# A graph network's 64-channel table, made for two blocks of nodes at once from unsplit fp32 instead of one block from split bf16

## The chip, the cores and the metric

The kernel runs on one core of one Trainium2 chip. The metric is device time in microseconds (us): the median of three runs, of which the lowest and the highest are also given. One execution was taken with the hardware profiler; every row below is from it.

## The reference, cut to what matters

Four graph layers on 6250 nodes and 100000 edges (`src`, `dst`, sorted by `dst`). The change touches two things that the first and the last layer compute:

```
# layer 0, second convolution: b has 64 channels
agg = segment_sum(b[src], dst)            # "the second sum"
h   = relu((b + agg) @ W1b + b1b) ...
# layer 3, spline convolution of 64 channels, 125 weight matrices of 64 x 64
z        = einsum('ni,kio->nko', v, stn2_w)   # v: nodes x 64; z: nodes x 125 x 64
gathered = z[col*125 + idx]                   # 8 corners of a cell for each edge
out      = segment_sum(sum_s basis * gathered, row) / degree + stn2_b
```

`z` does not depend on the second sum. It is written to HBM as a table, in which cells that are read together lie together, and gathered in a later stage.

## The kernel before

Nodes lie in 49 blocks of 128 (NB), edges in 832 tiles of 128 slots, 8 tiles to a group (T), 104 groups (G), 4 groups to a quad. Every stage is a block of five instruction streams with hand-set semaphores; there is no scheduler, and each engine runs its stream in the written order. All stages follow one another with a barrier between them.

The stage of the change is `second_sum_phase`. It does two jobs side by side:

- **The second sum.** GpSimd (POOL) gathers 128 rows of 384 bytes for each tile by an indirect DMA (L1560) and then issues a small memset (L150). It may gather group g+3 once VectorE has copied that group's indices, which VectorE does (`indices.put`) after it has added the sums of group g-1 into `dest`. TensorE sums a group with 24 bf16 products against one-hot matrices (`sums`, L1641). So gathers run at most some three groups ahead of the sums.
- **The 64-channel table** (`Table`, called `other`). For one block, VectorE splits the fp32 features into three bf16 terms (`three`, 5 instructions), TensorE transposes four stacks of them (`flip`, L1435), ScalarE (ACT) copies these out of PSUM (L1424), and TensorE makes the table in 25 parts of 320 columns: five bf16 products add up to one part in one of five PSUM banks (`multiply`, L1451). ACT copies each part to a staging buffer `z` (L1417); after five parts SyncE (SP) stores a piece of 960 KB (L1370). There are two `z` buffers, and ACT waits until the store of two pieces ago has landed.

TensorE's order for a pair of blocks is: 24 loop rounds, each with flip, 12 parts, sums, 13 parts, sums, and the same again for the other block; so one quad of the sum goes with one pair of blocks. Then come the last block's 25 parts and the sums of the last two quads (groups 96 to 103).

The weights are prepared far earlier, in the sorter's second stage (`place_phase`). There POOL scatters rows with indirect DMAs (L656), VectorE ranks the edges, and at the end of each of its 49 rounds splits a slice of the weights into bf16 terms (`HalfWeights.split`); after the last round SP stores them to HBM (L361 for the 64-channel ones).

Of the kernel before, what the change touches and what calls it, by code (L numbers as in the profile page):

```python
# [297 lines left out]
class HalfWeights:  # L298
# [6 lines left out]
    def __init__(self, k, stn2_w, conv_w, tent_w):  # L305
        self.of = stn2_w, conv_w, tent_w
        self.wide = [dram(k, "wide_w", [LO, self.WIDE], BF16) for _ in range(2)]
        self.slim = dram(k, "slim_w", [LO, self.SLIM + self.TENT], BF16)

    def hold(self, k):  # L310

        self.step_wide, self.step_slim = (-(-n // SPLIT_STEPS) for n in (self.WIDE, self.SLIM + self.TENT))
        self.raw_wide = sb(k, None, "raw_wide", [LO, self.step_wide * SPLIT_STEPS])
        self.raw_slim = sb(k, None, "raw_slim", [LO, self.step_slim * SPLIT_STEPS])
# [3 lines left out]
    def load(self, eng, sem):  # L318
        stn2_w, conv_w, tent_w = self.of
        for n in range(2):  # L320
            to = self.raw_wide[n * D_HID:(n + 1) * D_HID, 0:self.WIDE]
# [8 lines left out]
    def clear(self, dve):  # L330
        dve.memset(self.raw_wide[:, self.WIDE:], 0.0)
# [3 lines left out]
    def parts(self, k, ph):  # L335
        self.halves = [sb(k, ph, "halves", [LO, self.step_wide * SPLIT_STEPS], BF16) for _ in range(2)]
        self.thirds = sb(k, ph, "thirds", [LO, self.step_slim * SPLIT_STEPS], BF16)
# [3 lines left out]
    def split(self, dve, c, i):  # L341
        wide, slim = bass.ds(i * self.step_wide, self.step_wide), bass.ds(i * self.step_slim, self.step_slim)
        w, first, third = self.raw_wide[:, wide], self.halves[0][:, wide], self.halves[1][:, wide]
        v, u = self.raw_slim[:, slim], self.thirds[:, slim]
# [12 lines left out]
        return as_is(dve, u[last_], v[last_])  # L357

    def store(self, eng, sem):
        for n in range(2):  # L360
            eng.dma_start(self.wide[n], self.halves[n][:, 0:self.WIDE]).then_inc(sem, 16)  # L361
        eng.dma_start(self.slim, self.thirds[:, 0:self.SLIM + self.TENT]).then_inc(sem, 16)

    STORES = 16 * 3
# [4 lines left out]
class Sorter:  # L369


    def __init__(self, k):
# [5 lines left out]
        k.halves.hold(k)  # L378
# [19 lines left out]
def load_phase(k, s, src, dst, uv, uvw, s_rows):  # L398
    nc = k.nc
    with phase(nc) as ph:  # L400
# [9 lines left out]
        with nc.Block() as block:  # L410
            @block.sync
            def _(sp):
# [6 lines left out]
                k.halves.load(sp, weighed)  # L419
                sp.wait_ge(weighed, 16 * HalfWeights.LOADS)  # L420
# [12 lines left out]
            def _(dve):  # L433
# [9 lines left out]
                k.halves.clear(dve)  # L443
# [86 lines left out]
def place_phase(k, s, carried, s_rows, d_rows):  # L530
# [3 lines left out]
    with phase(nc) as ph:  # L534
# [8 lines left out]
        k.halves.parts(k, ph)  # L543
# [9 lines left out]
        with nc.Block() as block:  # L553
            @block.vector
            def _(dve):
# [4 lines left out]
                with dve.Fori(0, pairs) as i:  # L560
                    c.enter(i, 2 * 8 + HalfWeights.STEPS)
# [19 lines left out]
                    k.halves.split(dve, c, i).then_inc(split, 1)  # L581
# [39 lines left out]
            def _(sp):  # L621
# [19 lines left out]
                k.halves.store(sp, stored)  # L641
                sp.wait_ge(stored, HalfWeights.STORES)

# [653 lines left out]
class Table:  # L1297
# [8 lines left out]
    def __init__(self, k, ph, src, K, weights, C, rows, side, wide, piece, table, tail=None, shared=False, banks=5, zs=2):  # L1306
# [16 lines left out]
        self.stacks = (0, LO, 2 * LO, K) if K == D_HID else (0, LO, 2 * LO)  # L1323
        self.weights_of = weights
        self.weights = [sb(k, ph, "weights", [LO, rows * side * C], BF16) for _ in weights]
        if K == D_HID:
            first, third = self.weights
            self.terms = ((0, first, LO), (1, first, LO), (2, first, LO), (3, third, LO), (2, third, K))
        else:
            self.terms = tuple((n, self.weights[0], LO) for n in range(3))  # L1330
# [183 lines left out]

class Convolution:
# [3 lines left out]
    def __init__(self, k, K, C):  # L1519
        self.K, self.C = K, C  # L1520
        self.table = dram(k, "corners", [NN * self.CELLS * 25 * self.WIDE, C])

# [43 lines left out]
def second_sum_phase(k, table, dest, making):  # L1566
# [3 lines left out]
    with phase(nc) as ph:  # L1570
# [7 lines left out]
        other = Table(k, ph, *making)  # L1578
        with nc.Block() as block:
# [11 lines left out]
            def _(dve):  # L1591
                c = Chain(dve, own)
                indices.first(dve)
                for n in range(2):
                    other.three(dve, c, other.src[:, n, :], n)
# [13 lines left out]
                def block_ahead(i, b):  # L1609

# [1037 lines left out]
```

## Time and profile before

| | us |
|---|---|
| median of the three runs (lowest, highest) | 11980.05 (11966.1, 11993.72) |
| profiled execution: first to last instruction (span) | 11729.7 |
| median less span | 250.35 |
| stage of the second sum, 3079 to 4648 us of the span | 1569 |
| the same stage: TensorE busy, ACT busy, POOL busy | 1319.9, 574.6, 1032.9 |

The page gives no time of its own for the profiled execution, only its span; what lies outside first and last instruction is taken as the 250.35 us by which the median is longer. Busy times of a stage are to be read against its 1569 us: TensorE is busy for 84% of it, POOL for 66%, ACT for 37%. Busy time of TensorE holds matmuls whose ends are modelled, so the start-to-start distances of groups are the surer measure, and they are used below. Over the whole span TensorE's granted clock averages 0.605 of full speed; in this stage it is 0.87.

### The profile page before, as it was taken

To read this page: it belongs to the slowest core of one execution; us is meant where nothing else is said; L and a number is where in the kernel's file an instruction comes from. 1 tells how busy PE (TensorE), PEld (TensorE's weight loads), DVE (VectorE), ACT (ScalarE), POOL (GpSimd) and SP (SyncE) were. 2 spreads that over 40 slices of the span, in tenths; PEclk is the share of its full clock that TensorE was granted. 3 is DMA by queue.
4 is the path that set the end of the run, shared out by engine and by line. 5 is a ranking of instruction groups with operands and counts; after the bars stand their busy time and mean duration, and the time that the engine had idled before them with its cause. 6 is when DMAs were issued, how large, how long until landed. Compare 5 with 4: busy or idle time off the path is not lost. (4 is left out here: it accounts for less than half of the span.)

```text
span 11729.7 us, 173426 instructions
## 1 busy us (share of the span) xinstructions
PE 6194.3 (53%) x40278; PEld 4754.9 (41%) x40279; DVE 6868.2 (59%) x17651; ACT 2989.3 (25%) x7270; POOL 7301.5 (62%) x10729
## 2 busy tenths in 40 slices
PE   4333244444688987666664555555544444662332
PEld 3222244434344443355553555555523333332222
DVE  6555666664322222577787666666656767655555
ACT  0000022221233332111112555555531111220000
POOL 3888788882366665577773333333327877228887
PEclk8555555555688987566665555555565555685555
DMA  6332222224455554222325777777621111587777
GB/s 195 113 113 57 62 62 62 63 62 131 149 190 187 193 186 134 52 74 74 78 77 147 281 285 278 280 284 281 235 81 43 44 41 43 178 323 219 221 222 199
DMA packets 894930, 1760.69 MB, mean 150 GB/s; under 512 B 487010, under 2 KB 487319, under 8 KB 889928
## 3 DMA queue, kind: packets, MB, share of 16 engines
q0 software_dynamic: 317952, 1023.05, 28.3%
q1 hardware_dynamic: 537672, 598.27, 15.2%
q10 hardware_dynamic: 39168, 138.04, 3.0%
q14 instruction: 113, 0.93, 0.0%
q8 instruction: 25, 0.41, 0.0%
HBM read 1150.36 MB, written 611.50 MB: 150 GB/s over the span
## 5 line engine op out<-in xcount | busy, mean ns | idle before, releaser
L1560 POOL DMA_INDIRECT got<-corners,now x1664 | 1679.5, 1009 | 1926.6 <-DVE now L1548 1171.3
L1560 POOL DMA_INDIRECT got<-node_rows,now x1664 | 1639.6, 985 | 1267.3 <-issue 1251.5
L1451 PE MATMUL made_p<-weights,turned 128*128 128x320 bf16 (+4 forms) x7595 | 1541.8, 334 | 203.0 <-ACT z L1417 106.6
L150 POOL MEMSET spare<- 128x192 f32 x4944 | 1376.4, 278 | 3.1
L2342 PE MATMUL sum_p<-msg_s,hot_s 128*128 128x64 f32 x3328 | 734.2, 422 | 931.6 <-DVE msg_s L1824 931.6
L1560 POOL DMA_INDIRECT got<-patches,now x832 | 839.3, 1009 | 565.4 <-DVE now L1548 283.0
L2342 PEld LDWEIGHTS sum_p<-msg_s,hot_s 128*128 128x128 f32 x3328 | 717.7, 332 | 937.5 <-issue 937.5
L1451 PEld LDWEIGHTS made_p<-weights,turned 128*128 128x128 bf16 (+1 forms) x7595 | 657.9, 101 | 1039.0 <-issue 517.0
L896 POOL DMA_INDIRECT d_rows<-row x832 | 942.9, 1133 | 184.3 <-issue 160.1
L1417 ACT COPY z<-made_p 128x384 f32<-128x384 f32 (+3 forms) x1495 | 714.6, 515 | 932.3 <-PE made_p L1451 612.1
L656 POOL DMA_INDIRECT s_rows<-row_now,pos_i x784 | 848.1, 1082 | 155.2 <-issue 136.5
L1606 DVE TENSOR_TENSOR a<-a,sum_p 128x64 f32 x832 | 184.0, 221 | 1124.4 <-remote 638.0
L1897 PE MATMUL acc_p<-msg,hot_s 128*128 128x32 f32 x1664 | 376.2, 402 | 873.2 <-DVE msg L1841 647.7
L1817 DVE TENSOR_TENSOR got<-got,weight 128x1024 f32<-128x1024 f32 x416 | 481.7, 1220 | 442.0 <-DMA d_rows<-row 422.9
L1897 PEld LDWEIGHTS acc_p<-msg,hot_s 128*128 128x128 f32 x1664 | 362.8, 330 | 887.4 <-issue 887.4
L593 PE MATMUL rank_p<-one,before 128*128 128x100 bf16 x784 | 186.1, 282 | 813.9 <-DVE one L383 743.4
L1831 DVE TENSOR_TENSOR got<-got,spline_w 128x512 f32<-128x512 f32 x416 | 260.8, 688 | 561.9 <-DMA got<-corners,now 561.9
L2441 ACT ACTIVATE prod<-prod,below,alpha 128x32 f32<-128x32 f32 x1664 | 516.4, 398 | 0.0
L864 PE MATMUL sum_p<-basis,hot_s 128*128 128x126 f32 x1664 | 388.2, 427 | 192.0 <-DVE basis L826 192.0
L2425 ACT ACTIVATE hot_d<-column,lo_now 128x128 f32<-128x128 f32 x840 | 256.8, 388 | 889.5 <-PE acc_p L2322 488.7
L864 PEld LDWEIGHTS sum_p<-basis,hot_s 128*128 128x128 f32 x1664 | 359.9, 328 | 211.3 <-DVE basis L826 211.3
L2322 PE MATMUL acc_p<-msg_d,hot_d 128*128 128x32 f32 x1680 | 377.2, 400 | 111.6 <-issue 56.1
(411 smaller groups left out, 13596.3 us busy)
## 6 DMA issues: line engine op xcount, KB each, us to landing
corners<-z SPq DMA_DIRECT2D x245, 960.0 KB
corners<-z SPq DMA_DIRECT2D x98, 864.0 KB
d_rows<-empty ACTq DMA_DIRECT2D x32, 1586.0 KB
row<-d_rows SPq DMA_DIRECT2D x104, 488.0 KB
corners<-z SPq DMA_DIRECT2D x49, 672.0 KB
s_rows<-empty ACTq DMA_DIRECT2D x32, 962.0 KB
row<-s_rows SPq DMA_DIRECT2D x104, 296.0 KB
got<-node_rows,now POOLq DMA_INDIRECT x1664
```

The source lines that it names most:

```text
L150: pool.memset(self.of[:, t, :], 0.0).then_inc(self.cleared, 1)
L656: pool.indirect_dma_start(out=s_rows, out_offset=bass.IndirectOffsetOnAxis(ap=pos_i[b][:, t, 0:1], axis=0), in_=row_now[b][:, t, :], in_of ...
L864: m = nc.tensor.matmul(part(b2, t), hot_s[b2][:, t, :], basis[b2][:, t, :], start=True, stop=True)
L896: pool.indirect_dma_start(out=d_rows, out_offset=bass.IndirectOffsetOnAxis(ap=to[:, t, DPOS:DPOS + 1], axis=0), in_=row[b][:, t, :], in_of ...
L1417: copy(to, of).then_inc(self.out[taker], 1)
L1451: m = nc.tensor.matmul(self.made_p[s % banks][:, 0:w], self.turned[b][0:rows, stack, :], weight[0:rows, at:at + w], start=n == 0, stop=n = ...
L1560: pool.indirect_dma_start(out=to[b][:, t, :], out_offset=None, in_=table, in_offset=bass.IndirectOffsetOnAxis(ap=indices.now[b][:, t:t + 1 ...
L1817: m = dve.tensor_tensor(v, v, last(weights[:, :, 2 * n:2 * n + 2], C), ALU.mult)
L1897: m = nc.tensor.matmul(at_block(acc, block_of(k, pe, t)), hot_s[b2][:, t, :], msg[b2][:, t, :], start=False, stop=False)
L2322: m = nc.tensor.matmul(at_block(acc, block_of(k, pe, t)), hot_d[b2][:, t, :], msg_d[b2][:, t, :], start=False, stop=False)
L2342: m = nc.tensor.matmul(sum_p[b2][:, t, :], hot_s[b2][:, t, :], msg_s[:, n, t, :], start=n == 0, stop=n == 1)
L2441: m = nc.scalar.activation(at[:, n, :], at[:, n, :], ACT.Exp, bias=below[b2][:, n:n + 1], scale=alpha[b2][:, n:n + 1])
```

## The change

`Table` for 64 channels is replaced in this stage by a new class, `PairTable`. Two blocks are taken at once: VectorE copies both blocks' fp32 features side by side (one instruction for ten), one fp32 transpose puts block 0 on partitions 0 to 63 and block 1 on 64 to 127, and each part of each block is then one fp32 product over 64 rows, block 0 from the lower half and block 1 from the upper half, the two in turn. There are four PSUM banks and four `z` buffers; ACT takes part q of block 0, then of block 1. A pair has 50 products instead of 250, 50 ACT copies as before, and 10 stores of 960 KB as before. The weights are kept in fp32, on both halves: the same 4 MB. The other tables (32 channels) keep `Table`.

```diff
 class TableWeights:                      # was HalfWeights
     def split(self, dve, c, i):          # the 64-channel weights are no longer split
-        as_is(dve, first, w)
         c.after(as_is(dve, u, v))
-        dve.tensor_tensor(w, w, first, ALU.subtract)
         c.after(dve.tensor_tensor(v, v, u, ALU.subtract))
-        as_is(dve, third, w)
         as_is(dve, u[second], v[second])
         c.after(as_is(dve, u[last_], v[last_]))
-        as_is(dve, first[D_HID:], third[D_HID:])
-        dve.tensor_tensor(w, w, third, ALU.subtract)
         c.after(dve.tensor_tensor(v[last_], v[last_], u[last_], ALU.subtract))
-        as_is(dve, third, w)
         return as_is(dve, u[last_], v[last_])
...
                         features(i * 2 + b, b, lambda each: T)
+                k.table_w.store_wide(sp, stored)
                 for b in range(2):
...
+class PairTable:
+    PAIRS, PARTS = NB // 2, 25
+    STEPS = 2 * PARTS
+    BANKS, ZS, PIECE = 4, 4, 5
+    BEFORE = (48, 49, 46, 47)
...
+    def store(self, sp, i, blocks=2):
+        cells, unit, rows = self.cells, self.unit, self.PIECE
+        for h, j in self.pieces(blocks):
+            z = (2 * h + j) % self.ZS
+            sp.wait_ge(self.out, i * self.STEPS + (self.STEPS + self.at(h * rows + rows - 1, j, blocks) + 1))
...
+    def pair(self, dve, i):
+        dve.sem_inc(self.seen, 1)
+        dve.tensor_copy(self.now[:], self.src[:, bass.ds(i * 2, 2), :]).then_inc(self.taken, 1)
...
+    def flip(self, pe, i):
+        pe.wait_ge(self.taken, i + 1)
+        pe.sem_inc(self.ready, 1)
+        pe.wait_ge(self.copied, i)
+        of = self.now[:].rearrange("p a k -> p (a k)")
+        self.k.nc.tensor.transpose(self.turned_p[:], of, self.k.ident[:]).then_inc(self.flipped, 1)
+
+    def multiply(self, pe, i, parts, blocks=2):
+        nc, K = self.k.nc, self.K
+        if parts[0] == 0:
+            pe.wait_ge(self.copied, i + 1)
+            pe.sem_inc(self.ready, 1)
+        for q in parts:
+            for j in range(blocks):
+                s = 2 * q + j
+                had = self.STEPS + self.at(q - 2, j, blocks) if q >= 2 else self.BEFORE[s]
+                pe.wait_ge(self.out, i * self.STEPS + (had + 1))
+                rows = slice(j * K, (j + 1) * K)
+                nc.tensor.matmul(self.made_p[s % self.BANKS][:, 0:self.col], self.turned[rows, :],
+                                 self.weights[rows, q * self.col:(q + 1) * self.col], start=True, stop=True).then_inc(self.made, 1)
...
+    def take(self, act, i, blocks=2):
+        C, cells, unit, rows = self.C, self.cells, self.unit, self.PIECE
+        for q, j in self.steps(blocks):
+            h, r = q // rows, q % rows
+            n = 2 * h + j
+            z = self.z[n % self.ZS]
+            if r == 0:
+                act.wait_ge(self.stored[n % self.ZS], i * (16 * self.uses(n % self.ZS)) + 16 * (n // self.ZS))
+                act.sem_inc(self.waited, 1)
+            act.wait_ge(self.made, i * self.STEPS + (self.at(q, j, blocks) + 1))
...
+            self.k.nc.scalar.copy(to, of).then_inc(self.out, 1)
...
 def second_sum_phase(k, table, dest, making):
-        other = Table(k, ph, *making)
+        other = PairTable(k, ph, *making)
...
             def _(pe):
...
-                half = other.parts // 2
-                with pe.Fori(0, NB // 2) as i:
-                    for b in range(2):
-                        n = i * 2 + b
-                        other.flip(pe, n + 1, 1 - b)
-                        other.multiply(pe, n, b, i, range(0, half))
-                        sums(pe, i, b * 2)
-                        other.multiply(pe, n, b, i, range(half, other.parts))
-                        sums(pe, i, b * 2 + 1)
-                other.multiply(pe, NB - 1, 0, NB // 2, range(other.parts))
+                quarters = (0, 7, 13, 19, other.PARTS)
+                with pe.Fori(0, other.PAIRS) as i:
+                    for b in range(4):
+                        other.multiply(pe, i, range(quarters[b], quarters[b + 1]))
+                        if b == 3:
+                            other.flip(pe, i + 1)
+                        sums(pe, i, b)
+                other.multiply(pe, other.PAIRS, range(other.PARTS), 1)
```

How the instructions move is shown by three places of the streams. First TensorE before, at the start of a loop round: `turned_p` are the transposes, `made_p_4488` to `made_p_4492` the five banks.

```order
L1435 MATMUL turned_p<-ident_53,now 128x128 x4
L1448 ISA
L1451 MATMUL made_p_4488<-weights,turned 128x320 x5
L1448 REGISTER_ALU
L1451 MATMUL made_p_4489<-weights,turned 128x320 x5
L1448 REGISTER_ALU
L1451 MATMUL made_p_4490<-weights,turned 128x320 x5
```

And TensorE after, where the first quarter of a pair ends and a group's sums (`sum_p`) follow:

```order
L1603 REGISTER_ALU
L1605 MATMUL made_p_4455<-weights,turned 128x320
L1760 ISA
L124 REGISTER_ALU
L1764 MATMUL sum_p_4422<-got,hot_d 128x64 x24
L1603 REGISTER_ALU
L1605 MATMUL made_p_4456<-weights,turned 128x320
```

A wait now stands before every single product where it stood before five, and the products go round four banks; the sums stand after 14, 12, 12 and 12 products of a pair.

VectorE before, in the last round's code (`now` and `rest` hold the split, `hot_d` the one-hot matrices of the next group):

```order
L1543 COPY now<-src_d 128x8
L1386 CAST now<-v 128x128
L1387 TENSOR_TENSOR rest<-v,now 128x64
L1388 CAST now<-rest 128x128
L1389 TENSOR_TENSOR rest<-rest,now 128x64
L1390 CAST now<-rest 128x128
L228 TENSOR_TENSOR hot_d<-column,lo_d 128x1024
```

VectorE after, in the loop:

```order
L1674 COPY now<-src_d 128x8
L1577 REGISTER_ALU
L1573 ISA
L1573 COPY now<-v 128x128
L228 ISA
L228 TENSOR_TENSOR hot_d<-column,lo_d 128x1024
```

Five instructions have become one, and it comes once in four groups instead of once in two.

SP in the sorter's second stage, before and then after, around the store of the weights (`row_now` are the feature loads of the last two groups):

```order
L627 DMA row_now<-in_edge_attr_2x_dram 80x8x64
L627 DMA row_now<-in_edge_attr_2x_dram 48x8x64
L627 DMA row_now<-in_edge_attr_2x_dram 80x6x64
L627 DMA row_now<-in_edge_attr_2x_dram 48x4x64
L361 DMA wide_w<-halves 128x8000 x2
L362 DMA slim_w<-thirds 128x4512
```

```order
L351 DMA wide_w<-raw_wide 128x8000
L619 DMA row_now<-in_edge_attr_2x_dram 80x8x64
L619 DMA row_now<-in_edge_attr_2x_dram 48x8x64
L619 DMA row_now<-in_edge_attr_2x_dram 80x6x64
L619 DMA row_now<-in_edge_attr_2x_dram 48x4x64
```

The 4 MB of 64-channel weights are now stored ahead of the last two groups' feature loads instead of behind them.

## Rows read from the trace of the kernel before

**Rows 1.** Windows of the second-sum stage: length, busy of each engine (instructions), clock, DMA.

```profile
3079.00:4648.00 1569.00, 1319.91 (x8818) 610.28 (x8818) 387.14 (x1297) 574.55 (x1274) 1032.93 (x1664) 0.87 0.54 182
```

**Rows 2.** Lines by form of that stage: busy us, mean ns, idle before, releasers.

```profile
L1451 PE MATMUL made_p<-weights,turned 128*128 128x320 bf16 x4900 | 974.9, 325 | 159.7 <-ACT z L1417 82.4 <-issue 77.1
L1417 ACT COPY z<-made_p 128x384 f32<-128x384 f32 x1225 | 548.4, 488 | 760.2 <-PE made_p L1451 522.0 <-DMA d_rows<-row 119.4 <-DMA corners<-z 70.4
L1560 POOL DMA_INDIRECT got<-node_rows,now x832 | 805.8, 968 | 889.0 <-issue 887.2 <-POOL spare L150 1.6 <-DMA got<-node_rows,now 0.2
```

**Rows 3.** Waits, 3090 to 4600, ACT and POOL: us in total, times, longest.

```profile
ACT z L1417 <- PE made_p L1451: 522.0, 585, 5.9
...
POOL got L1560 <- issue: 514.5, 797, 11.6
```

**Rows 4.** Timeline, one block in the middle: start, us, engine, line, what.

```profile
4046.92 0.87 PE L1641 MATMUL sum_p<-got,hot_d 128*128 128x64 bf16 x24
...
4047.99 9.45 SPq L1370 DMA_DIRECT2D corners<-z  x2
...
4051.77 0.59 ACT L1424 COPY turned<-turned_p 128x512 bf16<-128x512 bf16 x1 [4.27 <-DMA d_rows<-row]
...
4054.63 2.90 ACT L1417 COPY z<-made_p 128x384 f32<-128x384 f32 x7 [2.27 <-DMA d_rows<-row]
...
4055.16 2.97 PE L1451 MATMUL made_p<-weights,turned 128*128 128x320 bf16 x14 [2.81 <-ACT z L1417]
```

**Rows 5.** Timeline, start and end of the stage (27 calls of L1560 apart, then 29).

```profile
3081.26 1.04 POOL L1560 DMA_INDIRECT got<-node_rows,now  x1 [368.49 <-issue]
...
3094.18 12.36 PE L1451 MATMUL made_p<-weights,turned 128*128 128x320 bf16 x60
...
3119.63 0.95 POOL L1560 DMA_INDIRECT got<-node_rows,now  x1 [0.17 <-issue]
...
4560.35 22.27 PE L1451 MATMUL made_p<-weights,turned 128*128 128x320 bf16 x125
...
4591.35 0.95 POOL L1560 DMA_INDIRECT got<-node_rows,now  x1 [0.16 <-issue]
...
4634.08 0.95 POOL L1560 DMA_INDIRECT got<-node_rows,now  x1 [0.17 <-issue]
...
4641.87 1.46 PE L1641 MATMUL sum_p<-got,hot_d 128*128 128x64 bf16 x24 [11.46 <-DMA got<-node_rows,now]
...
4648.10 3.43 DVE L1234 TENSOR_TENSOR a<-a,b 128x3136 f32<-128x3136 f32 x1 [1.15 <-PEq L79]
```

**Rows 6.** Timeline of TensorE in two dense stages: products of fp32, two records each.

```profile
4661.83 1.17 PE L1098 MATMUL made_p<-stage,weight 128*128 128x256 f32 x2
4662.79 0.64 PE L1083 MATMUL in_p<-ident,a 128*128 128x128 f32 x2
...
4727.89 2.08 PE L1109 MATMUL out_p<-weight,stage 128*128 128x512 f32 x2
4729.75 0.42 PE L1083 MATMUL in_p<-ident,h 128*128 128x128 f32 x1
...
4727.89 0.50 PEld L1109 LDWEIGHTS out_p<-weight,stage 128*128 128x128 f32 x2 [1.50 <-issue]
```

**Rows 7.** Windows of the dense stages and of a later table stage.

```profile
4660.00:4670.00 10.00, 9.59 (x31) 6.93 (x30) 0.86 (x3) 2.31 (x7) 0.00 (x0) 0.50 0.00 0
4729.00:4739.00 10.00, 9.29 (x12) 2.59 (x11) 1.38 (x2) 0.53 (x2) 0.00 (x0) 0.50 0.00 0
10200.00:10300.00 100.00, 87.94 (x469) 42.93 (x470) 63.19 (x150) 46.74 (x87) 0.00 (x0) 0.97 0.97 384
```

**Rows 8.** The page: the rows that the sorter scatters.

```profile
L656 POOL DMA_INDIRECT s_rows<-row_now,pos_i x784 | 848.1, 1082 | 155.2 <-issue 136.5
```

**Rows 9.** Timeline, the end of that stage.

```profile
1339.24 0.83 SPq L361 DMA_DIRECT2D wide_w<-halves  x2
...
1357.73 0.27 POOL L150 MEMSET spare<- 128x192 f32 x1
```

More of the change, by code:

```diff
@@ L377, in __init__ @@
         self.run = sb(k, None, "run", [LO, 2 * KEYS])
-        k.halves.hold(k)
+        k.table_w.hold(k)
     def one_hots(self, k, dve, g, b):
@@ L418, in _ @@
                 sp.wait_ge(loaded, 128)
-                k.halves.load(sp, weighed)
-                sp.wait_ge(weighed, 16 * HalfWeights.LOADS)
+                k.table_w.load(sp, weighed)
+                sp.wait_ge(weighed, 16 * TableWeights.LOADS)
             @block.scalar
@@ L442, in _ @@
                 dve.memset(s.key[:, NE:, :], 0.0)
-                k.halves.clear(dve)
+                k.table_w.clear(dve)
                 dve.wait_ge(loaded, 128)
@@ L542, in place_phase @@
         empty = sb(k, ph, "empty", [LO, FILL, D_W])
-        k.halves.parts(k, ph)
+        k.table_w.parts(k, ph)
         hot, ranked, own, placed, headed, seen, fetched, drawn, filled, split, stored = ph.sems(
@@ L640, in _ @@
                 sp.wait_ge(split, pairs)
-                k.halves.store(sp, stored)
-                sp.wait_ge(stored, HalfWeights.STORES)
+                k.table_w.store_slim(sp, stored)
+                sp.wait_ge(stored, TableWeights.STORES)
             @block.gpsimd
@@ L1322, in __init__ @@
         self.copies = LO // K
-        self.stacks = (0, LO, 2 * LO, K) if K == D_HID else (0, LO, 2 * LO)
+        self.stacks = (0, LO, 2 * LO)
         self.weights_of = weights
         self.weights = [sb(k, ph, "weights", [LO, rows * side * C], BF16) for _ in weights]
[L1326 to L1330, printed above, removed]
+        self.terms = tuple((n, self.weights[0], LO) for n in range(3))
         self.now = [sb(k, ph, "now", [LO, 3, self.copies, K], BF16) for _ in range(2)]
@@ L1521, in __init__, with making_pairs @@
         self.table = dram(k, "corners", [NN * self.CELLS * 25 * self.WIDE, C])
+    def making_pairs(self, h, weights):
+        return h, weights, self.C, self.WIDE, self.table
     def making(self, h, weights):
@@ L1593, in _ @@
                 indices.first(dve)
-                for n in range(2):
-                    other.three(dve, c, other.src[:, n, :], n)
+                other.pair(dve, 0)
                 c.after(dve.memset(dest[:], 0.0))
@@ L1647, in _ @@
                 other.sync(sp)
-                other.finish(sp)
             @block.tensor
@@ L1671, in _ @@
             def _(act):
-                other.begin_copies(act)
-                with act.Fori(0, NB // 2) as i:
-                    for b in range(2):
-                        other.scalar(act, i * 2 + b, b, i)
-                other.scalar(act, NB - 1, 0, NB // 2, more=False)
+                other.scalar(act)
 def tent_phase(k, table, t16, dest):
@@ L2540, in last_layers @@
             table = dram(k, "patches", [NN * 12, 2 * D_IN + 4])
-            table_phase(k, h, D_IN, [k.halves.slim[:, HalfWeights.SLIM:]], D_IN, 4, 4, 2, 1, table, tail=t32[:, :, 0:4])
+            table_phase(k, h, D_IN, [k.table_w.slim[:, TableWeights.SLIM:]], D_IN, 4, 4, 2, 1, table, tail=t32[:, :, 0:4])
             t16 = sb(k, None, "t16", [LO, NB, D_IN], BF16)
@@ L2547, in last_layers @@
             with layer(k):
-                table_phase(k, *conv.making(h, [k.halves.slim[:, 0:HalfWeights.SLIM]]), shared=True, banks=7, zs=3)
+                table_phase(k, *conv.making(h, [k.table_w.slim[:, 0:TableWeights.SLIM]]), shared=True, banks=7, zs=3)
         spline_phase(k, conv, y)
@@ L2575, in program @@
         }
-        k.halves = HalfWeights(k, stn2_w, conv_w, tent_w)
+        k.table_w = TableWeights(k, stn2_w, conv_w, tent_w)
         k.of_src, k.of_dst = (sb(k, None, n, [1, LEAD + G * T + T], I32) for n in ("of_src", "of_dst"))
```

124 lines of the change are left out of this document (89 added, 35 removed).

## The prediction, made before the result was known

> **What bounds the kernel now.** I read the page's shares first (no engine is busy throughout, and its slices change from stage to stage, so each stage has its own limit), then the windows of the one stage that the change rewrites, its groups by line, its waits, and the timeline inside it. The reader is to see this. The stage lasts 1569 us at a mean granted clock of 0.87 [rows 1]. POOL, which gathers, is idle for 889 of them, nearly all with no releaser [rows 2, 3]: it waits for indices, which come only after sums that stand behind table parts in TensorE's stream. Left alone, it needs 1.42 us a tile: 27 calls from 3081.26 to 3119.63 [rows 5], 38.37 / 27. For 832 tiles that is 1182 us. So the sum alone would take three quarters of the stage, and the rest is the table's. Inside the table, ACT waits 522 us for finished parts [rows 3], so TensorE leads; the pace is 61.1 us for a pair of blocks, from the first part at 3094.18 to the last block at 4560.35 over 24 rounds [rows 5]. At the full clock the last block's 125 products take 22.27 us [rows 5], 0.178 each, so a pair's 250 are 44.5 us; the other 16 or so are four sums, stretches at the low clock, and stops such as that at 4055.16, where TensorE waited 2.81 us for a bank, because ACT came to its copies at 4054.63, after the store issued at 4047.99 had landed [rows 4].
>
> **The change part by part.** The stage's end is built from the pace P of a pair: 3094.2 (start of the parts) + 24 P + last block + tail. The tail is what follows the last block now: 4648.10 - 4560.35 - 22.27 = 65.5 us [rows 5]. It consists of the gathers and sums of the last groups, which the change leaves alone. P is the slowest of four.
>
> TensorE. The trace has no fp32 product of 320 columns over 64 rows; the nearest are 256 columns in 0.96 us start to start and 512 in 1.86 [rows 6], both while the granted clock stood at 0.50, that is 1.2 GHz [rows 7]. Between them lies 0.96 + 64/256 x 0.90 = 1.19, say 1.2 us at 1.2 GHz (pro rata from 512 it is 1.16). These stages are also the evidence on the clock: TensorE was busy for 9.59 and 9.29 of 10 us and was still granted 0.50 [rows 7]. Their biases are products over one row, so they are not pure, but I take 1.2 GHz for the new stream too. If the halves overlap fully, block 0 and block 1 share those 1.2 us, and 25 parts are 30 us. Add four sums at the low clock, 1.46 us each [rows 5], 5.8; the fp32 transpose with its copy, about 0.7; together 36.5. After sums, ACT's next copy comes late: sums at 4046.92, copy at 4051.77, 4.85 us [rows 4]. TensorE covers 1.46 of that with the sums and, with four banks, two parts of each block (2.4); the remaining 1.0, four times, makes it 40.5. If they do not overlap, 50 products are 60 us. Both ends are kept: 36.5 and 66.5.
>
> A rule of the Trainium skill bears on this. The rows show only products of one height at a time, so no overlap [rows 2, 6]. "TensorE: Matmul & The Clock Gate", Part 3 (The mechanism), states that products in different row groups run at the same time, and measures 3.07 times for four of them at 512 columns; by it the pair's products would be the 30 us. The same section says that weights load beside a running product only where the row group differs. That speaks against the change, and its consequence is priced as a rival below. No row here can show either.
>
> POOL. 1.42 us a tile at the start; 1.47 at the end (29 calls in 42.73 us, from 4591.35 to 4634.08) [rows 5]. The stretch comes with VectorE's one-hot beside it, once a group. The mean of the two, 8 x 1.448 = 11.58 us a group, gives 46.3 us a quad; the ends are 45.5 and 47.2. No gather is removed.
>
> ACT. 50 copies x 0.488 = 24.4 us [rows 2], below both.
>
> Staging and stores. Issue 4047.99 to ACT free at 4054.63 is 6.6 us for a store's round trip [rows 4]; 960 KB at the 384 GB/s of a later table stage [rows 7] is 2.6 us. Two pieces now fill together in 5 x 1.2 us and are stored one behind the other: (6.0 + 6.6 + 2.6) / 2 = 7.6 us per two pieces, 38 a pair. Bytes: the share is 0.54 over 1569 us [rows 1]; over 1222 us it is 0.69, and 0.97 has been reached [rows 7].
>
> So P = 46.3: POOL becomes the bound, ahead of TensorE's 40.5. The last block is now 25 products with nothing beside them, 25 x 1.2 = 30 us instead of 22.3; it delays the sums of group 96, while POOL has up to three groups of 11.6 in hand, so I charge the whole 30. End: 3094.2 + 24 x 46.3 + 30 + 65.5 = 4300.9, against 4648.1: 347 us less.
>
> The sorter's second stage. VectorE loses six small instructions a round of 16 tiles that POOL sets: 784 scatters of 1.082 us with 0.2 idle [rows 8]. That hides them, and the gain is taken as nothing. A call of L1560 takes 0.968 [rows 2]; if all of the difference came from VectorE's work beside it, it would be 784 x 0.114 = 89 us, but of that work the six are a small part (two groups a round bring eight operations over 800 columns), so I keep 9 us of it for the lower end at most. The weight store was issued at 1339.24 while POOL worked until 1358 [rows 9]: already hidden, so moving it gains nothing. It now runs ahead of the last feature loads; 4 MB at 384 GB/s are 11 us, about one group of scatters, which covers it. If uncovered, it costs up to 11. The load of the weights at the stage's start is the same 4 MB, and TensorE's wait for it stays.
>
> Sum: 11729.7 - 347 = 11382.6 for the span; with the 250.35 us around it, 11633 us, against the median of 11980.
>
> **The rivals.**
>
> *No overlap (the change does not do what it says).* The halves run one after the other, at 1.2 GHz. For it: no row shows two at once, and an fp32 product comes as two records [rows 6], which gives the sequencer more to order. Against: the operands and banks are distinct. P = 60 + 5.8 + 0.7 = 66.5, above 61.1: end 3094.2 + 1596 + 30 + 65.5 = 4785.7, 138 us later, 12118; with the 4 us of stops counted, 12214. The stage gets slower as soon as a part of both blocks takes over 2.2 us ((61.1 - 6.5) / 25, less a little for the last block).
>
> *Half overlap.* The second record of a product loads its weights only when the first is through. Two loads of an fp32 product take 0.50 us [rows 6], so a part of both blocks is 1.2 + 0.5 = 1.7, and P = 42.5 + 6.5 = 49.0: TensorE just passes POOL. End 3094.2 + 1176 + 42.5 + 65.5 = 4378.2: 270 less, 11710. Against it: from 256 to 512 columns a product grows by 3.5 ns a column [rows 6], 4.2 cycles of 1.2 GHz; at that rate 512 columns are 1.80 of the 1.86 measured, so little of its two loads is exposed.
>
> *No overlap, but full clock.* 50 products of 0.6 are 30 us again, POOL sets the pace, and the time is the forecast's. The trace of [rows 7] speaks against.
>
> *Stops.* With a wait before each product and ACT, stores and gathers out of step, P may be 50 to 58, as now it is 16 above the products: 11720 to 11910.
>
> **How the numbers follow.** Forecast (overlap, POOL's pace) 0.60; half overlap 0.13; full clock without overlap 0.04; stops 0.08; no overlap 0.15. The forecast's own range is 11595 (POOL at 45.5, last block hidden) to 11670. From 11580 to 11790 lie the forecast, half overlap, full clock, and the better third of stops: just 8 in 10. About 0.2% (24 us) is what a measurement of this kernel can tell from no change. Faster by more: all but the last case and a bit, 0.83; slower 0.14; same 0.03.
>
> **What would show it.** In the changed profile the stage should end near 4300 us, POOL be busy for over 0.85 of the time between its first and last gather, with calls 1.4 us apart; matmul starts on the two halves should lie closer than 1.2 us, with a part of both in 1.2; the granted clock should be near 0.5. The sorter's second stage should end where it did, within 5 us. A part of both blocks at 2.4 us and POOL busy near 0.6 would prove it wrong; so would TensorE waiting for ACT for more than 5 us a pair, though with less loss.

## The result, and the profile after

The changed kernel takes 11814.19 us (median of 4 runs, 11803.29 to 11822.42), the kernel before 11986.88 (4 runs, 11966.1 to 11995.87): ratio 0.9838, 95% interval 0.9805 to 0.9871. It is 173 us faster, half of the 347 that were forecast, and outside the range.

The windows of the whole stage come first (columns as in [rows 1]), to be held against 1569 us at clock 0.87.

```profile
3093.00:4591.00 1498.00, 939.49 (x4971) 575.33 (x4972) 335.03 (x1077) 537.40 (x1250) 1044.16 (x1664) 0.66 0.56 191
```

The groups by line of the same stretch answer to [rows 2]; the waits answer to [rows 3].

```profile
L1605 PE MATMUL made_p<-weights,turned 64*128 64x320 f32 x2450 | 825.5, 651 | 503.1 <-issue 261.1 <-ACT z L1629 210.8 <-ACT turned L1614 16.5
L1691 POOL DMA_INDIRECT got<-node_rows,now x832 | 817.1, 982 | 806.2 <-issue 798.6 <-POOL spare L150 7.0 <-DVE now L1674 0.7
L1629 ACT COPY z<-made_p 128x384 f32<-128x384 f32 x1225 | 531.6, 485 | 890.8 <-DMA d_rows<-row 394.5 <-PE made_p L1605 366.2 <-DMA corners<-z 98.5
```

```profile
DVE a L1736 <- remote: 657.1, 56, 25.5
ACT z L1629 <- DMA d_rows<-row: 394.5, 120, 14.6
ACT z L1629 <- PE made_p L1605: 366.2, 422, 12.9
```

POOL was to be the bound and is idle for 806 us. TensorE is busy for 939 of 1498 us and makes its products at a lower clock, 0.66. The stage's pace, from the first copy of `turned` at 3094.89 to the one at 4493.01, over 24 pairs:

```profile
3094.89 0.27 ACT L1634 COPY turned<-turned_p 128x128 f32<-128x128 f32 x1 [16.75 <-PE turned_p L1591]
...
4493.01 0.26 ACT L1614 COPY turned<-turned_p 64x128 f32<-64x128 f32 x1
...
4500.32 25.31 PE L1605 MATMUL made_p<-weights,turned 64*128 64x320 f32 x46 [5.59 <-issue]
```

That is 58.3 us a pair where 46.3 were forecast. (It includes the wait for the weights ahead of the first product. From the first product at 3106.61 to the first of the last block at 4493.42, the count that the prediction used, it is 57.8.) The last block takes 32.2 us where 30 were forecast: the group shown holds 46 of its 50 records, and the 5.59 us ahead of it are a stop. The overlap of the two halves is there. At a granted clock of 0.50 (first fence) ACT gets the two copies of a part every 1.07 us, the second fence:

```profile
4050.00:4054.00 4.00, 4.00 (x17) 3.62 (x15) 2.03 (x5) 3.00 (x9) 1.24 (x3) 0.50 0.00 0
```

```profile
4050.76 0.86 ACT L1629 COPY z<-made_p 128x384 f32<-128x384 f32 x2 [0.38 <-PE made_p L1605]
...
4051.83 0.86 ACT L1629 COPY z<-made_p 128x384 f32<-128x384 f32 x2 [0.21 <-PE made_p L1605]
...
4052.90 0.86 ACT L1629 COPY z<-made_p 128x384 f32<-128x384 f32 x2 [0.21 <-PE made_p L1605]
```

What eats it is seen 30 us earlier, in the timeline around a group's sums. It answers to [rows 4].

```profile
4018.38 0.87 PE L1764 MATMUL sum_p<-got,hot_d 128*128 128x64 bf16 x24
...
4019.18 1.63 PE L1605 MATMUL made_p<-weights,turned 64*128 64x320 f32 x6
4019.47 0.48 ACT L1629 COPY z<-made_p 128x384 f32<-128x384 f32 x1 [1.12 <-PE made_p L1605]
...
4020.97 0.48 ACT L1629 COPY z<-made_p 128x384 f32<-128x384 f32 x1 [1.02 <-PE made_p L1605]
...
4021.50 0.80 PE L1605 MATMUL made_p<-weights,turned 64*128 64x320 f32 x2 [0.69 <-ACT z L1629]
...
4031.13 0.48 ACT L1629 COPY z<-made_p 128x384 f32<-128x384 f32 x1 [9.68 <-DMA d_rows<-row]
...
4031.66 1.43 PE L1605 MATMUL made_p<-weights,turned 64*128 64x320 f32 x2 [9.36 <-issue]
...
4031.95 0.22 DVE L1736 TENSOR_TENSOR a<-a,sum_p 128x64 f32 x1 [12.90 <-remote]
```

The sums end by the record at 4019.25, and VectorE, which waits only for them, starts to add at 4031.95. ACT gets its next product as late. TensorE fills the banks that are free and then stands. The releaser that the profile names for ACT, a DMA into `d_rows`, belongs to another stage: the view has attached a wait that it can't place. The semaphore events in the trace show what it is. From the recorded end of a group's sums to the next update of their semaphore it is 4.4 us on average here (4.1 over the 101 of 104 sums that have an update of their own), and 1.2 us for the products (an upper bound, since 1078 updates are recorded for 1225 products; over those with an update of their own it is 0.45); in the kernel before, 3.1 and 1.0. I call these late reports.

They are TensorE's alone. Of ACT's copies and VectorE's adds a third have no update of their own on record, and all others have it 0.01 us after their end. TensorE starts 0.05 us (median) after the copy it waits for, as at 4021.50 above. POOL starts 1.17 us after VectorE's copy of the indices, here and in e17, where nothing is late. TensorE's ends are modelled, so this can be TensorE finishing late as well as a report that travels late. In this profile ACT never took a product behind a sum before that sum's update (94 sums), so the two can't be told apart here.

### The profile page after: what moved, and what is told of

It is laid out like the page before. It is cut to its first block and busy times, and to the rows that moved or that the text cites. A ratio compares the mean times of both kernels' runs of the same rounds, so it can differ in the third digit from the quotient of the medians.

```text
span 11820.6 us, 164571 instructions
## 1 busy us (share of the span) xinstructions
PE 5828.4 (49%) x36294; PEld 4733.7 (40%) x36433; DVE 6740.8 (57%) x17136; ACT 2952.2 (25%) x7246; POOL 7285.4 (62%) x10729
## 2 busy tenths in 40 slices
DMA packets 894641, 1760.67 MB, mean 149 GB/s; under 512 B 486978, under 2 KB 487287, under 8 KB 889896
## 3 DMA queue, kind: packets, MB, share of 16 engines
q0 software_dynamic: 317952, 1023.05, 28.1%
## 5 line engine op out<-in xcount | busy, mean ns | idle before, releaser
L1605 PE MATMUL made_p<-weights,turned 64*128 64x320 f32 x2450 | 825.5, 651 | 503.1 <-issue 261.1
L1605 PEld LDWEIGHTS made_p<-weights,turned 64*128 64x128 f32 x2450 | 464.7, 262 | 796.8 <-issue 425.3
L1629 ACT COPY z<-made_p 128x384 f32<-128x384 f32 x1225 | 531.6, 485 | 890.8 <-DMA d_rows<-row 394.5
```

The costliest lines, as they stand in the source:

```text
L1605: nc.tensor.matmul(self.made_p[s % self.BANKS][:, 0:self.col], self.turned[rows, :], self.weights[rows, q * self.col:(q + 1) * self.col], ...
L1629: self.k.nc.scalar.copy(to, of).then_inc(self.out, 1)
```

## The experiments

Kernels sent together ran on one chip, beside the kernel before. The sets differ far more than the change does, so a label's number comes with its set: in set A (e1 to e4) the kernel before took 12011 us, in B (e5 to e8) 10743, in C (e9 to e12) 11720, in D (e13 to e16) 12057, in E (e17, e18) 10765. Each set is one chip at one time, so what is said of a chip below can't be told from what is said of its time. "Prompt" means that reports are not late; that holds for B and E.

The pace of the changed kernel and its variants is the distance from first to last copy of `turned`, for a pair of blocks. The kernel before transposes one block ahead, so its pace is counted from its first product to the first one of the last block: 61.1 us in the first profile, 64.9 in e1, 62.5 in e10, 48.0 in e17. Where the two kernels are compared, the changed one is counted in that way as well: 57.8 in the result's profile, 56.5 in e9, 45.9 in e18.

**e1, e10, e17: the kernel before, profiled again.** Nothing edited.

> The kernel before, unchanged, profiled once more, to see how steady its stages are. Theory 1 (the first profiled execution, span 11729.7, was a fast one in its unchanged stages): the second sum's stage is 1569 us again within 5, the score stage is near 1596 instead of 1542 and the message stage near 2220 instead of 2172, as in the changed kernel, and the span is near 11970. Theory 2 (the change itself lengthens the later stages): all stages repeat within 5 us, and the span is near 11730.

> The kernel before, profiled on the same chip as the run above, so that stages can be compared one by one. Theory E: where it takes some 10740 in all, its pace is 58 to 62 us a pair; sums are reported within 0.1 us. The sorter's stage ends within 5 us of where it ends in the changed kernel if its edits are hidden, 15 to 40 us earlier if they are not.

> The kernel before, profiled again beside the kernel below. Where reports are late (time near 12000) its last scatter of the sorter's stage was issued at 1348.1 and 1356.8 so far, and that of the changed kernel and its variants at 1365 to 1396. If that is the change's doing, this run gives 1345 to 1360 again; if it is chance between executions, it may give up to 1396. On other chips 1354 to 1358 for both.

Lengths of stages in us. The first row ends at the first product on `sums`, the first node update. The second sum is counted from the later update's first product on `y` to the next one on `a`, so it holds that update as well. Scores and messages end where the next stage begins, tent and spline with their last product; the stages in between are left out.

| stage | first profile | before A, e1 | after, result | after D, e13 | before C, e10 | after C, e9 | before E, e17 | e18, E |
|---|---|---|---|---|---|---|---|---|
| up to the node update | 2718.0 | 2712.6 | 2733.0 | 2753.6 | 2716.4 | 2718.2 | 2717.9 | 2716.0 |
| second sum | 1641.7 | 1738.3 | 1571.0 | 1568.0 | 1676.7 | 1537.3 | 1328.3 | 1290.2 |
| scores | 1541.9 | 1606.4 | 1595.6 | 1534.7 | 1466.8 | 1492.7 | 1409.1 | 1396.1 |
| messages | 2172.6 | 2220.2 | 2219.4 | 2218.1 | 2175.1 | 2181.7 | 1788.9 | 1788.8 |
| tent | 1386.0 | 1457.8 | 1427.7 | 1452.7 | 1381.5 | 1377.4 | 1248.4 | 1249.0 |
| spline | 1251.1 | 1257.6 | 1258.4 | 1252.9 | 1248.6 | 1250.9 | 1252.3 | 1255.4 |

Theory 1 of e1 holds for scores and messages (1606.4 and 2220.2) but not for the second sum, which was to repeat within 5 us and is 97 longer; and its reason is another. The first profile looks like one from C's condition (messages 2173 and tent 1386, as in e10), and the times beside it are like A's. Nothing lies "around the span": e1 took 12011.18 with a span of 12009.4. And the stage that the change rewrites is 1738 us in A, 1677 in C and 1328 in E, for the same code.

In E reports are prompt: 0.03 us on average for the products, and for the sums of the messages' stage 0.01 us where A, C and D have 4.6 to 4.9. The windows and a group of the kernel before there (e17):

```profile
3081.00:4266.00 1185.00, 1172.01 (x8614) 571.20 (x8611) 366.27 (x1211) 613.68 (x1271) 996.80 (x1600) 0.99 0.68 238
```

```profile
L1451 PE MATMUL made_p<-weights,turned 128*128 128x320 bf16 (+1 forms) x6114 | 1094.6, 303 | 0.0
```

TensorE is busy for 1172 of 1185 us at clock 0.99 and its pace is 48.0. Of the 16.6 us a pair above the products that I had read as sums, low clock and stops of the design (61.1 - 44.5), 3.5 are left here. The other 13 come with late reports, as stops and as a lower clock (0.87).

**e2: five banks instead of four.**

```
-    BANKS, ZS, PIECE = 4, 4, 5
+    BANKS, ZS, PIECE = 5, 4, 5
```

> The changed kernel with five banks for its products instead of four (PSUM has one left). Theory A (after each sum the next free bank is reported late, and four banks cover only two parts): one more product of each two is covered, four times a pair, 0.5 us each, and the low clock after each stop is shorter: pace 58.1 to about 55, stage 50 to 80 us shorter, time 11740 to 11765. Theory B (stores that hold back the gathers and with them the sums): the banks change nothing, pace 58 within 0.5, time within 15 us of the changed kernel.

Measured: 11822.34 us (4 runs), ratio 0.9845 (0.9808 to 0.9881), pace 58.3, as the changed kernel's. Theory A is wrong: a fifth bank covers half a microsecond, and reports are late by many times that (a sum's by 4.9 us on average in e2).

**e3: no gathers in the stage; e4: no stores in step with it.**

```
-                        gather(pool, got, table, indices, i, b, gathered, spare)
```

> The changed kernel without the gathers of the second sum's stage (the sums read zeros that VectorE wrote once, and wait only for their one-hots). Theory B (gathers that come late because stores hold their packets): the stops go away and the pace is that of TensorE and the staging, 33 to 40 us a pair, stage near 950 to 1000. Theory A (the bank cover after the sums is too thin, whoever feeds them): stops of 2 to 5 us remain after each sum, pace 44 to 50.

```
-            sp.dma_start(...).then_inc(self.stored[z], 16)
+            sp.sem_inc(self.stored[z], 16)
```

> The changed kernel without the stores of the table's pieces in step with the products (the table is filled with zeros ahead of the first product, some 630 us, and staging buffers are free at once). From the first product on: theory B (stores hold back gathers and staging) gives the pace of POOL, 46 to 47 us a pair. Theory A gives 55 to 58.

Without gathers: 32.8 us a pair, every one of TensorE's reports within 0.1 us, and the clock is back at 0.89 (0.66 with the gathers):

```profile
3116.00:3902.00 786.00, 638.36 (x4703) 426.49 (x4703) 307.63 (x986) 490.13 (x1222) 0.00 (x0) 0.89 0.75 300
```

```profile
L1605 PE MATMUL made_p<-weights,turned 64*128 64x320 f32 x2400 | 562.9, 517 | 147.9 <-ACT z L1629 133.6 <-DMA weights<-wide_w 7.9 <-issue 4.5
```

Without stores: 54.8 us a pair over the 23 pairs behind the fill, sums reported 3.2 us late. Over its last 23 pairs the changed kernel has 56.9. So the stores are worth 2 us of the 57, the gathers 25; theory B, by which the pace without stores is POOL's 46 to 47, is wrong as well.

**e5, e14: gathers as they are, but nobody reads them.**

```
-                gathered.wait(pe, b, i + 1)
...
-... got[b][:, t, n * D_HID:(n + 1) * D_HID],
+... nothing[:, t, n * D_HID:(n + 1) * D_HID],
```

> The changed kernel with all gathers of the second sum's stage issued as they are, but the sums read zeros from another buffer and do not wait for them (VectorE waits for a landing before it lets the buffer be gathered anew). Theory C (TensorE stands still because the sums wait for rows that land late): the pace falls from 57 to that of the kernel without gathers, 32 to 36 us a pair, or to POOL's 46 if that is then the bound, and the records of TensorE's semaphores follow the ends of its products at once (0.0 us, as without gathers). Theory D (work of the gathers delays what TensorE, ACT and VectorE report to each other, whoever reads the rows): the pace stays 52 to 58, and sums are reported 3 to 4 us after their end.

> The kernel of the unread gathers again, for a chip on which reports are late. Theory C (TensorE's sums wait for rows that land late): the pace is 44 to 47 us, POOL's. Theory D (the gathers delay the reports of others, whoever reads the rows): 52 to 57 us, and the products' reports are still late by 1 us on average. On a prompt chip it repeats 45.6.

In B, where reports are prompt anyway: 45.6, POOL's own pace, which decides nothing. In D: 58.5, the same as the changed kernel beside it (58.3) and a little above the 52 to 57 expected, products reported late by 1.35 us on average. e14's row reads like the changed kernel's own (0.67 and 0.56 in e13 too):

```profile
3112.00:4517.00 1405.00, 895.66 (x4719) 545.09 (x4720) 312.42 (x987) 523.38 (x1224) 978.75 (x1569) 0.67 0.55 196
```

Theory C falls. D stands for TensorE and not for ACT and VectorE: the sums do not wait for rows; the gathers delay what TensorE reports, whoever reads the rows.

**e7, e15: a plain load of 128 rows in place of each gather; e6: small memsets on POOL.**

```
+                            pool.dma_start(got[b][:, t, :], table[t * LO:(t + 1) * LO, :]).then_inc(gathered.landing(b, t), 16)
```

> The changed kernel with a plain load of 128 rows of the same length, issued by POOL, in place of each indirect gather; sums wait for them and read them. Theory D2a (the descriptors that POOL works out for an indirect gather are the cost): the pace falls to 33 to 40 us and updates come at once. Theory D2b (any transfer of such rows, or its landing, delays the reports): the pace stays over 50.

> The kernel with plain loads of 128 rows in place of the indirect gathers again, for a chip on which reports are late. If it is the indirect gathers as such: 35 to 38 us a pair, all reports within 0.1 us, as on the prompt chip. If any traffic of POOL's does it: over 45 us, reports late.

> The changed kernel without gathers, with eight small memsets on POOL in place of each gather (about 1 to 1.4 us a tile, each of them reported by a semaphore). Theory D1 (POOL's engine work and its reports hold up the others): the pace is over 50 us a pair and updates are late. Theory D2 (the transfers, or the writing of their descriptors, do it): the pace is 32 to 34 us as without gathers, unless POOL's own work of 8 tiles times 4 bounds it, at most 46; updates at once.

The plain loads give 36.2 in B and 36.1 in D, on the chip where the gathers give 58.3, and every report comes within 0.1 us. From D:

```profile
3087.00:3953.00 866.00, 664.78 (x4708) 441.11 (x4709) 309.05 (x986) 495.71 (x1224) 578.78 (x1573) 0.85 0.85 318
```

```profile
L1721 POOL DMA_DIRECT2D got<-node_rows x787 | 424.5, 539 | 654.5 <-DVE now L1674 632.2 <-issue 15.8 <-POOL spare L150 5.8
```

So it is something about the indirect gather, not the landing of 48 KB a tile. Nor is it the number, size or queue of the packets: over the whole run e15 moves 894642 packets and e13 894641, with 317952 in the queue that the gathers use in both. POOL's share of busy time is near too, 0.67 in e15 and 0.70 in e14. Four differences aren't told apart: the gather is indirect; it reads scattered rows where the plain loads read neighbouring ones; the edit also drops POOL's wait for earlier landings; and a call takes 976 ns in e14 and 539 here. The memsets ran in B only, where nothing is late, and gave 32.9: on the theory they say nothing.

**e8, e16: both products of a part on one half.**

```
-                rows = slice(j * K, (j + 1) * K)
+                rows = slice(0, K)
```

> The changed kernel with both products of a part taken from the same half of TensorE (block 1 gets block 0's values), so that nothing can overlap. If the overlap is what the change lives on: products of a pair 50 x 1.07 at 1.2 GHz or 50 x 0.68 at 2.4 GHz, pace from 57 to 65 to 75 us a pair, stage 200 to 400 us longer, a part of both blocks in over 1.3 us at the full clock. If the stops set the pace and the overlap is hidden in them: pace within 3 us of 57.

> Both products of a part from one half of TensorE again. On a prompt chip it repeats 61.4 us a pair. On one with late reports the products of a pair take 53 us at the low clock and the stops come on top: 68 to 76 us a pair; if the stops were hidden behind the slower products: 62 to 64.

61.4 in B and 63.7 in D. In B TensorE is then hardly ever idle; the products of the two blocks come one by one, a copy each 1.07 us (clock 0.50):

```profile
3600.12 0.48 ACT L1629 COPY z<-made_p 128x384 f32<-128x384 f32 x1 [0.59 <-PE made_p L1605]
3601.18 0.48 ACT L1629 COPY z<-made_p 128x384 f32<-128x384 f32 x1 [0.59 <-PE made_p L1605]
```

```profile
L1605 PE MATMUL made_p<-weights,turned 64*128 64x320 f32 x2400 | 1323.4, 744 | 17.6 <-DMA weights<-wide_w 11.7 <-ACT z L1629 5.4
```

The overlap is thus worth 61.4 - 46.3 (e18) = 15 us a pair where reports are prompt and POOL is the next bound, and 63.7 - 58.3 = 5.4 where they are late. Its first expectation (65 to 75) was too high.

**e9, e13: the changed kernel again; e18: with the six VectorE instructions kept.** e18's edit puts the split of the wide weights back into the sorter's stage, into buffers that nobody reads.

```
+        as_is(dve, first, w)
+        dve.tensor_tensor(left, w, first, ALU.subtract)
+        as_is(dve, third, left)
+        as_is(dve, first[D_HID:], third[D_HID:])
+        dve.tensor_tensor(left, left, third, ALU.subtract)
+        as_is(dve, third, left)
```

> The changed kernel itself once more, because the kernel before took 12011 us on the chip of the first four experiments and 10743 on that of the next, where reports of semaphores come at once with all gathers in place. Theory E (the forecast's mechanism holds where reports are prompt): on a chip on which the kernel before takes some 10740, the pace is POOL's, 45 to 48 us a pair, the second sum's stage 300 to 350 us shorter than in the kernel before, and the time 0.967 to 0.972 of it. On a chip on which the kernel before takes some 12000, the pace is 57 again and the ratio 0.984. Theory F (the change is worth half of the forecast anywhere): ratio near 0.984 on either.

> The changed kernel on whatever chip comes, with the three below on the same one. On a chip on which reports are prompt (the kernel before takes some 10740): theory E gives POOL's pace, 45 to 48 us a pair, and a time 300 to 350 us below the kernel before; theory F gives 130 to 190 us. On one on which they are late: 55 to 58 us a pair again.

> The changed kernel with the six small VectorE instructions a round kept in the sorter's stage (they split the raw weights into buffers that nobody reads; the fp32 weights are still stored and used). Theory G (with fewer VectorE instructions between them, reports come at worse times in this stage, where they are late): the last scatter is back at 1345 to 1360. Theory H (it is where the weights are stored, ahead of the last feature loads, or chance): 1365 to 1396 where reports are late. Second sum's stage as in the changed kernel.

In C, which is neither of the two conditions that e9 foresaw: 11587.37 against 11720.02, ratio 0.9898 (0.9873 to 0.9923), pace 56.5 against 62.5. In D: 11826.18 (2 runs) against 12056.86, 0.9818 (0.9738 to 0.9898), pace 58.3. The changed kernel itself never came to a prompt chip; e18 did, in E, and in the second sum's stage it is the same code. There its pace is 46.3 (45.9 from product to product) and its stage 1290.2 us, against a forecast of 46.3 and, counted as in the table, 1641.7 - 347 = 1295. POOL is the bound, at 88% busy, with calls 1.39 us apart:

```profile
3078.00:4220.00 1142.00, 759.54 (x4779) 520.29 (x4779) 315.18 (x996) 505.21 (x1249) 1007.65 (x1581) 0.75 0.69 248
```

```profile
3603.02 0.95 POOL L1703 DMA_INDIRECT got<-node_rows,now  x1 [0.16 <-issue]
...
3604.41 0.95 POOL L1703 DMA_INDIRECT got<-node_rows,now  x1 [0.17 <-issue]
...
3605.79 0.95 POOL L1703 DMA_INDIRECT got<-node_rows,now  x1 [0.16 <-issue]
```

But the kernel before has 48.0 there and needs 1328.3 us for the stage. The gain is 38 us in the stage: 24 x 2.1 = 50 by the pace, less 13 at its end, where the last block and what follows are longer. The whole takes 10713.59 against 10763.26 and 10764.54, one run each (with e18's extra instructions). Theory E is right in the pace and wrong in the gain. F is wrong too: the ratio is 0.9838 in the result, 0.9898 in C and 0.995 in E.

**e11: six pieces a block; e12: besides, one copy for both blocks of a part.**

```
+    FROM = (0, 5, 9, 13, 17, 21, 25)
```

> The changed kernel with the 25 parts of a block stored as six pieces (5, 4, 4, 4, 4, 4) instead of five, so that the first piece of the next pair does not take the buffer that the last one has just filled. ACT waits 7.6 us a pair for stores in the run without gathers. If POOL sets the pace: within 0.1% of the changed kernel. If staging or late reports set it: 2 to 6 us a pair less, 50 to 150 us.

> Six pieces as above, and one copy by ACT for both blocks of a part (25 longer copies a pair instead of 50, and half the waits of TensorE), four banks in two pairs. If the number of reports that can be late is what costs (theory D): 57 falls to 50 to 54 us a pair, 80 to 150 us less. If it is the cover by banks alone: a little slower than six pieces, because a product waits for a copy of about 0.9 us; up to 30 us. If POOL sets the pace: within 0.2%.

In C: 11611.63 us, 0.9911 (0.989 to 0.9933), and 11589.47, 0.989 (0.9858 to 0.9921), against 11587.37 of the changed kernel: no difference that can be told. In e12's profile the second sum's stage is 29 us shorter than e9's (1508.4 against 1537.3), but its scores' stage is 31 longer, and such differences arise between executions of unchanged stages too. Halving the number of reports bought 1.5 us a pair, not 3 to 7, so their number costs little. No version here beats the changed kernel.

## Why the prediction was wrong, by its own steps

**What bounds the kernel now: the step that failed.** "The other 16 or so are four sums, stretches at the low clock, and stops" treated the 61.1 us of a pair as a property of the code. They are 48.0 where reports are prompt, 62.5 in C and 64.9 in A. I saw one late copy, 4.85 us, took it for the cost of having sums in between [rows 4] and didn't ask why a semaphore should take so long. A look at all of them would have shown 3.1 us for sums and 1.0 for products. So the step that failed is this one: POOL was made the bound at 46.3 us a pair, ahead of a TensorE at 40.5 that was charged 4 us for stops. TensorE with its stops took 57.8.

**TensorE, 40.5 a pair.** 1.2 us for a part of both blocks at 1.2 GHz: measured 1.07. Full overlap, by the Trainium skill's "TensorE: Matmul & The Clock Gate", Part 3: shown, by 1.07 us for two blocks against 2.14 in e8. Without gathers the pace is 32.8, below the 36.5 forecast without stops, with a granted clock of 0.89 where 0.5 was assumed. The term that was mis-sized is the "remaining 1.0, four times" for stops: it is 58.3 - 32.8 = 25.5 us and not 4. By rows: products' busy time is 825.5 / 24.5 = 33.7 us a pair against 562.9 / 24 = 23.5 without gathers, 10 us of lower clock (0.66 against 0.89); idle before them 503.1 / 24.5 = 20.5 against 147.9 / 24 = 6.2, 14 us of standing. Going from E to a late set costs the kernel before 14 to 17 us a pair (62.5 and 64.9 against 48.0). That the new code suffers more because it waits more often with less in hand (0.54 us of products in a bank, half of 1.07, against 5 x 0.178 = 0.9) is a guess that no run shows; a fifth bank (e2) and half the reports (e12) changed little. Where reports are prompt, POOL's bound covers 13 of the 25, so the changed kernel as a whole loses only 11 to 12 us from E to a late set (56.5 and 57.8 against 45.9).

**POOL, 46.3 as the bound.** Right in size (46.3 in E, 45.6 in e5), but it is the bound only where reports are prompt. In the result's profile it is busy for 0.70 of the stage where over 0.85 was forecast.

**ACT, staging, last block, tail.** ACT's copies stay at 0.485. Staging was no bound: no stores 54.8, six pieces no gain. The last block was charged 30: it took 27.0 in e18 and 32.2 with a stop in the result. The tail was 65.5 and is 65.7.

**The sum.** Taking 347 from one profile's span and adding "250.35 us around it" joined two conditions, a profile like C's and times like A's. By the sum's own terms, the stage ended at 4591.3 and not at 4300.9: 12 us for a later start, 24 x (57.8 - 46.3) = 276 for the pace, 2 for the last block and nothing for the tail. The second sum is 71 us shorter than in the first profile. Against e1, whose messages' stage is like the result's, it is 167 shorter (1738.3 to 1571.0; the two are of different sets), and 24 x (64.9 - 57.8) = 170 of pace account for that. So most of the measured 173 is this stage; the node update comes 20 us later than in e1, and scores and tent are 11 and 30 us shorter though nothing in them was changed. The lower end of the range, 11595, is 11584 by its own two terms, which changes nothing.

**The sorter's stage, nothing.** In C right: 2718.2 against 2716.4, last scatter within 4 us. E (2716.0 against 2717.9) tests only the store's place, since e18 keeps the split, and B has no profile of the kernel before. In the result's own profile the node update is reached 15 us later than in the first one, where 5 were allowed. There, in A and in D it is open: the changed kernel and its variants reach the node update at 2724.7 to 2761.1 (8 profiles), the kernel before at 2712.6 (one profile). The two kernels meant to decide it, e17 and e18, ran in a prompt set. So it may cost 12 to 49 us there, and neither its instructions nor the store's place is shown to be the cause.

**The rivals.** "Stops, P 50 to 58: 11720 to 11910", given 0.08, is what happened, with late reports as its mechanism. That the time fell inside its span is in part luck: by the sum, a pace of 57.8 would have given some 11910 and not 11814, because the base was wrong too. No overlap and half overlap are refuted by the 1.07 us.

**Open.** Why TensorE's reports are late on some chips and not on others, by what path an indirect gather delays them, and whether it is the report or TensorE's own work that is late. Whether something else on the chip plays a part can't be seen from one core's trace.

## What to carry to other kernels

Before a forecast takes a stop as part of the design, compare the recorded end of the releasing instruction with the start of the released one over the whole stage; where they lie apart by microseconds, as here, the stop may not belong to the code and may stay when the code is changed. Go by the waiting engine's start and not by the update's record: where records are missing, the next one looks like a late one. Check that profile and times come from the same condition: here every profiled run's span and own time agree within some 2 us, so a gap of 250 is a warning, not a constant. An engine that a change frees is worth only what the next bound leaves: here, in E, 48.0 to 45.9 us.

## What the runs showed of the hardware

- While indirect gathers run on POOL in this stage, TensorE's semaphore reports come late in the first two profiles and in A, C and D, and not in B and E: a sum's by 3.1 to 4.9 us on average (by up to 16.5 in the result's profile). ACT's and VectorE's don't: 0.05 us from a copy's end to the product that waits for it, and 1.17 us from VectorE's index copy to the gather, as in E. With plain loads or none, no report of the stage is late, in A (e3) and D (e15) too. The unchanged stages differ as well: messages take 2220 us in A and D, 2175 in C and 1789 in B and E.
- Products of fp32 with 64 rows on the two halves of TensorE overlap fully: 1.07 us for 320 columns of both at 1.2 GHz (the result's profile), 2.14 on one half (e8).
- The granted clock of this fp32 stream was 0.50 when TensorE hardly ever paused (e8, busy for 1456 of 1474 us), 0.89 without gathers, 0.75 with POOL as the bound and 0.66 with late reports. I had expected 0.5 throughout; I have no rule for it.
